# A six-block decoder kernel: order of the first transfers, waits at first use, and where the fp4 weights are turned

## The reference, cut to what matters

```python
x = _layernorm(x + _L0_attn_ref(x, Wq, Wk, Wv, Wo))            # causal self-attention with rope, 16 heads
x = _layernorm(x + _L0_xattn_ref(x, ctx, ...))                  # cross-attention, q and k normed per head
x = _layernorm(x + _L0_ffn_ref(x, w_gate, w_up, w_down))        # gated feed-forward, inputs and weights in fp4
x = _layernorm(x + _L1_attn_ref(x, ...))                        # linear attention, depthwise convolutions, MLP
x = _layernorm(x + _L1_xattn_ref(ctx, x, ...))                  # causal cross-attention
x = _layernorm(x + _L1_ffn_ref(x, ...))                         # 8 experts, top 2

def fp4_linear(x, w):                                           # inside _L0_ffn_ref
    return einsum('bsk,nk->bsn', fp4_quant_dequant(x), fp4_quant_dequant(w))   # per block of 16, along k
```

## Time and profile before

| | |
|---|---|
| median of 3 runs | 846.2 us (846.08 to 848.11) |
| the profiled execution | 849.09 us, its span 847.3 us |
| instructions | 13277 |
| PE busy | 663.4 us (78%) |
| DVE busy | 559.9 us (66%) |
| ACT busy | 350.0 us (41%) |
| POOL busy | 94.3 us (11%) |
| mean granted clock of PE | 0.894 |
| moved by DMA | 10.11 MB, 7.12 MB of it in the first 30 us |

### The profile page before, as it was taken

The page is one execution under the profiler, slowest core; times in us unless marked ns, Lnnn a source line. Parts: engine busy times, 40 slices in busy tenths (PEclk is TensorE's granted clock), DMA queues, the critical chain, the costliest instruction groups (busy, mean ns, idle before and its releaser), DMA issues.

```text
span 847.3 us, 13277 instructions
## 1 busy us (share of the span) xinstructions
PE 663.4 (78%) x5081; PEld 440.5 (52%) x5081; DVE 559.9 (66%) x1492; ACT 350.0 (41%) x568; POOL 94.3 (11%) x224
## 2 busy tenths in 40 slices
PE   1788479675889797999957965876668969889995
PEld 0557347443454374566635753564435436646663
DVE  6476667889676664554547685678967656465555
ACT  0653535221766552322227443622238546332220
POOL 0002100202102101000020020021120130100002
PEclk9999769677799898999989995796969989899998
DMA  9000100000000000000000000000000000000000
GB/s 320 17 2 14 37 1 2 0 1 0 2 1 1 1 2 1 1 1 0 1 28 2 2 1 1 2 1 1 0 2 1 1 0 2 2 0 1 1 1 25
DMA packets 8867, 10.11 MB, mean 12 GB/s; under 512 B 1240, under 2 KB 7776, under 8 KB 8288
## 3 DMA queue, kind: packets, MB, share of 16 engines
q1 hardware_dynamic: 8800, 9.22, 3.2%
HBM read 8.17 MB, written 1.05 MB: 11 GB/s over the span
## 4 chain that ended last, share of the span: by engine, by line
PE 60%; DVE 22%; ACT 11%; issue 4%; POOL 1%; another core or an unknown queue 0%; DMA 0%; SPq 0%; POOLq 0%; DVEq 0%
PE ps L780 14%; PE ps L542 8%; PE ps L771 6%; PE ps L479 6%; PE ps L498 5%; PE ps L465 2%; PE ps L725 2%; PE ps L730 2%; ACT s_k L857 2%; ACT s_probs L899 1%; DVE s_work L1060 1%; PE ps L553 1%; DVE s_r L1084 1%; PE ps L510 1%; ACT s_v L840 1%
## 5 line engine op out<-in xcount | busy, mean ns | idle before, releaser
L1011 ACT ACTIVATE s_k<-ps,eb 128x512 f32<-128x512 f32 x64 | 44.0, 687 | 136.0 <-PE ps L780 135.9
L1512 POOL TENSOR_TENSOR s_rs<-s_mv,eps 128x1 f32<-128x1 f32 x96 | 19.1, 201 | 640.1 <-DVE s_mv L1090 460.2
L1114 DVE TENSOR_REDUCE s_row_max<-ps 128x16 f32<-128x1024 f32 x48 | 58.6, 1221 | 46.8 <-PE ps L498 46.8
L1447 DVE SCALAR_TENSOR_TENSOR s_pT<-ps,eb,s_k 128x512 f32<-128x512 f32 x64 | 48.0, 749 | 57.0 <-ACT s_k L1011 53.7
L542 PE MATMUL ps<-s_v,s_pT 128*64 128x108 f32 x1536 | 82.0, 261 | 2.0 <-ACT s_headsT L890 1.7
L542 PEld LDWEIGHTS ps<-s_v,s_pT 128*64 128x64 f32 x1536 | 73.5, 138 | 11.9 <-issue 11.4
L879 ACT ACTIVATE s_pT<-ps 128x512 f32<-128x512 f32 x96 | 56.9, 595 | 51.0 <-PE ps L479 49.5
L479 PE MATMUL ps<-tabs,s_probs 128*128 128x128 f32 x384 | 64.8, 296 | 13.3 <-ACT s_probs L899 12.1
L771 PEld LDWEIGHTS ps<-wo,s_pT 128*128 128x128 f32 x512 | 61.7, 192 | 17.7 <-issue 12.4
L780 PE MATMUL ps<-s_xT,wg 128*128 128x512 f32 x128 | 69.5, 626 | 1.5 <-DVE s_pT L1447 1.1
L780 PE MATMUL ps<-s_xT,wu 128*128 128x512 f32 x128 | 68.9, 621 | 0.0
(11 more groups left out here) (220 smaller groups left out, 1130.5 us busy)
## 6 DMA issues: line engine op xcount, KB each, us to landing
mats<-in_mats SPq DMA_DIRECT2D x1, 1216.0 KB, 8.7
s_cin<-in_ctx SPq DMA_DIRECT2D x4, 256.0 KB, 4.2
s_xin<-in_x SPq DMA_DIRECT2D x4, 256.0 KB, 4.6
wg<-in_wg SPq DMA_DIRECT2D x1, 1024.0 KB
wu<-in_wu SPq DMA_DIRECT2D x1, 1024.0 KB
wo<-in_wo SPq DMA_DIRECT2D x1, 1024.0 KB
out_x<-s_x SPq DMA_DIRECT2D x4, 256.0 KB, 2.4
fc<-in_fc SPq DMA_DIRECT2D x2, 256.0 KB
```

The lines of the kernel that those rows point to most:

```text
L1011: act.activation(h.esg[:, n % 2, :], h.ps[:, 0, 0:TOK], ACT.Silu, bias=eb[:, 0, n:n + 1]).then_inc(h.e_silu, 1)
L1114: dve.tensor_reduce(h.row_max[:, t % 2, :], s3, AX, ALU.max).then_inc(h.max_here, 1)
L1447: dve.scalar_tensor_tensor(h.ehid[:, (n // 2) % 2, n % 2, :], h.ps[:, 1, 0:TOK], eb[:, 1, n:n + 1], h.esg[:, n % 2, :], ALU.add, ALU.mult) ...
```

## The change

- SP opens the pass before the transfers, and issues them in another order: `fp4_gu`, `tabs`, `cin` and `xin` of stream 0, the first 6 matrices (`MATS_FIRST`), `fp4_d`, `cin` and `xin` of stream 1, `identb`, mask, `cols`, the other 13 matrices, then the late ones. The bytes are the same.
- `late_here` and the shared counts are split into semaphores by use (`cols_here`, `more_mats_here`, `fp4_d_here`, `biases_here`, `fc_here`, `experts_here`), and each is awaited inside the loop where the data is first used. Ahead of the loop PE, ACT and DVE wait only for `tabs`, DVE also for the fp4 weights and POOL for `cols`.
- The nine transposes of the fp4 weights and ACT's three copies move into the loop, to the start of stream 0's feed-forward. They are executed in both passes.
- The fp4 weights get buffers of their own (their quantized form must last into the second pass).
- The memsets of `v2` and `hq` and the two sums for `cw1` move from DVE to POOL.

```diff
+            open_pass()
+            for h in streams:
+                sp.sem_inc(h.stored, 16)
+            sp.dma_start(fp4_gu[:, :], fp4_gu_in.rearrange("p c n -> p (c n)")).then_inc(fp4_here, 16)
+            sp.dma_start(tabs[:, :], tables_in).then_inc(tabs_here, 16)
+            load(0, 0)
+            sp.dma_start(mats[:, 0:MATS_FIRST, :], mats_in[:, 0:MATS_FIRST, :]).then_inc(mats_here, 16)
+            sp.dma_start(fp4_d[:, :], fp4_d_in).then_inc(fp4_d_here, 16)
+            load(0, 1)
+            sp.dma_start(identb[:, :], identb_in).then_inc(mask_here, 16)
+            sp.dma_start(cmask[:, :], cmask_in).then_inc(mask_here, 16)
+            sp.dma_start(cols[:, :], cols_in).then_inc(cols_here, 16)
+            sp.dma_start(mats[:, MATS_FIRST:, :], mats_in[:, MATS_FIRST:, :]).then_inc(more_mats_here, 16)
...
             def keys_ahead(h):
                 yield
+                pe.wait_ge(more_mats_here, 16)
...
+            def turn_fp4_weights(h):
+                pe.wait_ge(fp4_w_ready, 1)
+                for c in range(2 * KC):
+                    pe.transpose(h.ps[:, c // 4, tile(c % 4)], fp4_gu[:, tile(c)], ident)
+                for c in range(KC):
+                    ins = pe.transpose(h.ps[:, 2, tile(c)], fp4_d[:, tile(c)], ident)
+                ins.then_inc(fp4_w_turned, 1)
+
             def ffn(h):
+                if h is streams[0]:
+                    turn_fp4_weights(h)
                 yield
...
-            pe.wait_ge(tabs_here, 48)
-            pe.wait_ge(fp4_w_ready, 1)
-            for c in range(2 * KC):
-                pe.transpose(ps[:, c // 4, tile(c % 4)], fp4_gu[:, c, :], ident)
-            for c in range(KC):
-                ins = pe.transpose(ps[:, 2, tile(c)], fp4_d[:, tile(c)], ident)
-            ins.then_inc(fp4_w_turned, 1)
-            pe.wait_ge(fp4_w_here, 1)
-            pe.wait_ge(mask_here, 16)
-            pe.wait_ge(late_here, 16 * LATE)
+            pe.wait_ge(tabs_here, 16)
             with pe.Fori(0, PASSES):
...
+            def take_fp4_weights(h):
+                act.wait_ge(fp4_w_turned, 1)
+                act.activation(gu_w[:, 0:4 * P], h.ps[:, 0, :], ACT.Copy)
+                act.activation(gu_w[:, 4 * P:6 * P], h.ps[:, 1, 0:2 * P], ACT.Copy)
+                act.activation(d_w[:, :, :], h.ps[:, 2, 0:KC * P].rearrange("p (c n) -> p c n", n=P),
+                               ACT.Copy).then_inc(fp4_w_here, 1)
...
-            dve.wait_ge(fp4_here, 32)
+            dve.wait_ge(fp4_here, 16)
             at_once(ffn_weights(streams[0]))
-            dve.wait_ge(late_here, 16 * LATE)
+            dve.wait_ge(tabs_here, 16)
             with dve.Fori(0, PASSES):
...
             for h in streams:
+                pool.memset(h.v2_all[:, :, :], 0.0).then_inc(v_zeros_set, 1)
...
+            for h in streams:
+                pool.memset(h.hq[:, :, :], 0.0)
                 pool.memset(h.vz[:, :, :, :], 0.0).then_inc(zeros_set, 1)
+            pool.wait_ge(cols_here, 16)
...
-            pool.wait_ge(late_here, 16 * LATE)
```

More of the change, by code:

```diff
@@ L70 @@
 HEADS_NORM = 17
-LATE = 11
+MATS_FIRST = 6
 def steps(*names):
@@ L339, in decoder @@
         streams = [stream(k) for k in range(STREAMS)]
-        fp4_gu = placed(streams[1].k4, 0, 2 * KC, P)
-        fp4_d = placed(streams[1].k4, 2 * KC * P, FFN_PAD)
+        fp4_gu = sb("fp4_gu", [P, 2 * KC * P])
+        fp4_d = sb("fp4_d", [P, FFN_PAD])
         def col(name):
@@ L416, in open_pass @@
                     sp.sem_inc(t, 1)
-            sp.dma_start(tabs[:, :], tables_in).then_inc(tabs_here, 16)
-            sp.dma_start(cols[:, :], cols_in).then_inc(tabs_here, 16)
-            sp.dma_start(fp4_gu, fp4_gu_in).then_inc(fp4_here, 16)
-            sp.dma_start(fp4_d, fp4_d_in).then_inc(fp4_here, 16)
-            sp.dma_start(identb[:, :], identb_in).then_inc(tabs_here, 16)
-            for k in range(STREAMS):
-                load(0, k)
-            sp.dma_start(mats[:, :, :], mats_in).then_inc(mats_here, 16)
@@ L437, in _ @@
+            for dst, src in ((fc1[:, :], fc1_in), (fc1b[:, :], fc1b_in), (fc2[:, :, :], fc2_in)):
+                sp.dma_start(dst, src).then_inc(fc_here, 16)
+            for dst, src in ((router[:, :], router_in), (eb[:, :, :], eb_in), (wg[:, :, :], wg_in), (wu[:, :, :], wu_in),
+                             (wo[:, :, :], wo_in), (bout[:, :], bout_in)):
+                sp.dma_start(dst, src).then_inc(experts_here, 16)
             with sp.Fori(0, PASSES - 1) as c:
@@ L921, in cross_attention @@
                 yield from attention_tiles(h, 1)
+            def take_fp4_weights(h):
[4 more added lines that the diff above has]
+                               ACT.Copy).then_inc(fp4_w_here, 1)
             def ffn(h):
+                if h is streams[0]:
+                    take_fp4_weights(h)
                 yield from take_x(h, 3, 3)
@@ L1263, in ffn_weights @@
             def ffn_weights(h):
-                gu3 = fp4_gu.rearrange("p c (b k) -> p (c b) k", k=BLOCK)
+                gu3 = fp4_gu[:, :].rearrange("p (b k) -> p b k", k=BLOCK)
                 ins = yield from quantize(h, gu3, gu3, 2 * KC * P // BLOCK, once, 0)
@@ L1267, in ffn_weights @@
                 dve.wait_ge(once, 9)
-                d3 = fp4_d.rearrange("p (b k) -> p b k", k=BLOCK)
+                dve.wait_ge(fp4_d_here, 16)
+                d3 = fp4_d[:, :].rearrange("p (b k) -> p b k", k=BLOCK)
                 ins = yield from quantize(h, d3, d3, FFN_PAD // BLOCK, once, 9)
@@ L1481, in network @@
                 yield from experts(h)
-            for h in streams:
-                dve.memset(h.hq[:, :, :], 0.0)
-                dve.memset(h.v2_all[:, :, :], 0.0).then_inc(v_zeros_set, 1)
-            dve.wait_ge(v_zeros_set, 2)
-            for h in streams:
-                dve.memset(h.v2[0:S, :, 0::2, DK:DK + 1], 1.0)
-                ins = dve.memset(h.v2[S:P, :, 1::2, DK:DK + 1], 1.0)
-            ins.then_inc(v_ones_set, 1)
-            dve.wait_ge(tabs_here, 48)
-            dve.tensor_scalar(cw1[:, 0:1], col("cpe1_w1"), 1.0, None, ALU.add)
-            dve.tensor_scalar(cw1[:, 1:2], col("cpe2_w1"), 1.0, None, ALU.add).then_inc(conv_mids_set, 1)
-            dve.wait_ge(fp4_here, 32)
+            dve.wait_ge(fp4_here, 16)
             at_once(ffn_weights(streams[0]))
-            dve.wait_ge(late_here, 16 * LATE)
+            dve.wait_ge(tabs_here, 16)
             with dve.Fori(0, PASSES):
@@ L1553, in _ @@
             for h in streams:
+                pool.memset(h.v2_all[:, :, :], 0.0).then_inc(v_zeros_set, 1)
+            pool.wait_ge(v_zeros_set, 2)
+            for k, h in enumerate(streams):
+                pool.memset(h.v2[0:S, :, 0::2, DK:DK + 1], 1.0).then_inc(v_ones_set, 1)
+                pool.wait_ge(v_ones_set, 2 * k + 1)
+                pool.memset(h.v2[S:P, :, 1::2, DK:DK + 1], 1.0).then_inc(v_ones_set, 1)
+                pool.wait_ge(v_ones_set, 2 * k + 2)
+            for h in streams:
+                pool.memset(h.hq[:, :, :], 0.0)
                 pool.memset(h.vz[:, :, :, :], 0.0).then_inc(zeros_set, 1)
+            pool.wait_ge(cols_here, 16)
+            pool.tensor_scalar(cw1[:, 0:1], col("cpe1_w1"), 1.0, None, ALU.add)
+            pool.tensor_scalar(cw1[:, 1:2], col("cpe2_w1"), 1.0, None, ALU.add).then_inc(conv_mids_set, 1)
             pool.wait_ge(consts_set, 2)
-            pool.wait_ge(late_here, 16 * LATE)
             with pool.Fori(0, PASSES):
```

44 lines of the change are left out of this document (23 added, 21 removed).

## The result

The changed kernel takes **842.15 us** at the median (841.19 to 842.89, 4 runs), the kernel before on the same chip 847.15 (846.08 to 848.46, 4 runs): a ratio of 0.9936 with a 95% interval of 0.9923 to 0.9949. It is faster by 0.6%, where 833.4 was forecast, with a range of 829.5 to 839.5. The sign held and the size did not. 5 us came where 12.8 were expected.

The account below looks back on a forecast made before the run. PE was taken to carry 60% of the chain, with everything in the loop hanging on the rope product's start. From 847.3, -14.4 and +1.6 gave a span of 834.5, a median of 833.4 us; range 829.5 to 839.5.

Parts of the forecast that it names:

- Term 1: Start of the loop: without the waits ahead of it, rope product L1143 starts at 16.3 instead of 30.69, -14.4 us.
- the scale: Bytes landed against time in the kernel before, 220, 238 and 311 KB per us, used to date the new transfers.
- Rival A: Front: two DVE quantizing operations of 768 columns each wait for a POOL memset; start 1.2 later, 834.6 us; chance 0.12.
- Term 2: Nine transposes in the loop, ahead of stream 1's projection, delay it about 0.8 us a pass, twice: +1.6 us.
- Rival D: Loop: PE is granted less clock, its 508 us of chain lengthen in proportion; 859.7 us at 0.85; chance 0.03.
- B: Turn in the loop: PE is slow there, so it costs +4.0 us instead of +1.6, 835.8 us; chance 0.13.
- C: Near 23: instruction fetch held behind expert weights, 835 us; whole gain lost, 846 us; chance 0.02.

Follow-up runs that it names:

- before_turn_in: Kernel before with only the nine transposes and three copies moved into the loop, fp4 weights in own buffers, waits ahead of the loop kept: 849.15 us, ratio 1.001.
- after_third: The changed kernel unaltered, run once more: 841.15 us, ratio 0.992 to the kernel before.
- after_fill2: Changed kernel plus 80 unused PE transposes a pass, ahead of stream 1's first scores and in both cross-attentions, one wait moved earlier: 828.1 us.
- waits_in: Kernel before with the change's in-loop waits added on PE, ACT and DVE, those ahead of the loop kept: 850.0 us, ratio 1.001.

## Why the prediction was wrong

**Term 1, the front: right.** -14.4 was forecast and -14.05 came. The transfers landed 0.7 to 1.4 us later than the scale said, and DVE's ready time of 16.40 was 1.1 later than the 15.3 forecast; PE, with L591 done at 16.60, set the rope product all the same, nearly a tie. The mask, the memsets and the expert weights held nobody, as costed.

**Rival A's mechanism exists, in another place.** DVE and POOL in the kernel after:

```profile
5.13 1.33 DVE L1074 TENSOR_SCALAR s_qmax<-s_qmax 128x48 f32<-128x48 f32 x1
...
7.97 0.56 DVE L1084 TENSOR_SCALAR s_work<-s_work 128x768 int32<-128x768 int32 x1
```

```profile
4.78 0.96 POOL L1574 MEMSET s_vz<- 128x1024 f32 x1
5.67 0.74 POOL L1573 MEMSET s_hq<- 128x768 f32 x1
6.35 1.00 POOL L1574 MEMSET s_vz<- 128x1024 f32 x1
```

The kernel before has the first of these without POOL beside it:

```profile
7.54 0.19 DVE L1054 TENSOR_SCALAR s_qmax<-s_qmax 128x48 f32<-128x48 f32 x1
```

A tensor_scalar of 48 columns took 1.33 us in place of 0.19; the one of 768 columns that I feared for took its 0.56 at 7.97, when POOL was done (7.35). This is the 1.1 us that DVE was late, and it cost nothing only because PE was to come 1 us behind DVE and came 0.2 behind. The Trainium skill (SBUF — State Buffer, "SBUF: two separate sides") has a DVE operation in a two-port mode and a GpSimd operation take the shared ports in turn, the later one blocked for the whole instruction. The rows agree in part: L1074 starts at 5.13 beside the first memset above, which ends at 5.74, and itself ends at 6.46, just behind the second one's end at 6.41, so it outlasts one memset more than the one it met. The reciprocal and the product behind it, at 6.49 and 6.98 beside the third memset, take their usual 0.45 and 0.96. Whether L1074 runs in a two-port mode no row says.

**Term 2, the turn: mis-sized.** +1.6 was forecast, and the trace shows 0.25 us a pass at the place, 0.5 in all. The rows:

```profile
143.76 0.49 PE L516 MATMUL ps<-mats,s_headsT 128*128 128x128 f32 x2
...
144.09 0.82 PE L619 MATMUL ps<-tabs,fp_gu 128*128 128x128 f32 x6
...
144.75 0.49 PE L621 MATMUL ps<-tabs,fp_d 128*128 128x128 f32 x3
...
145.07 0.39 PE L516 MATMUL ps<-mats,s_headsT 128*128 128x128 f32 x2
145.27 0.60 ACT L939 ACTIVATE gu_w<-ps 128x512 f32<-128x512 f32 x1 [2.38 <-PE ps L621]
...
146.03 0.50 ACT L941 ACTIVATE d_w<-ps 128x384 f32<-128x384 f32 x1
...
146.40 0.30 ACT L904 ACTIVATE s_headsT<-ps 128x128 f32<-128x128 f32 x1
```

Stream 0's last projection starts at 143.76 here. From it to stream 1's are 145.07 - 143.76 = 1.31 us, and were 153.68 - 152.62 = 1.06 before; to the copy of stream 1's heads 146.40 - 143.76 = 2.64, and 155.01 - 152.62 = 2.39 before. So the turn makes stream 1 late by 0.25, not by 0.7 or 0.8: the nine transposes take 1.15 in place of 1.3 to 1.4, and at either end they overlap their neighbours by 0.15. At the end the profile of before_turn_in shows none of it, and the medians 0.8 to 1.4, with intervals that hold 0 as well as 1.6.

**The step that failed** is the sum itself: "inside the loop a delay on the chain moves everything behind it", and so a gain at the front was carried to the end unchanged, at an unchanged clock. Rival D had the mechanism and the right price, and got 0.03, because I asked of it only whether it could turn the sign. Its own formula, put on the medians: 508 us of chain on PE x (0.900 / 0.886 - 1) = 8.0 us. The loop grew by 819.6 - 812.7 = 6.9. With the 8.0 in it the sum gives 848.3 - 14.05 + 8.0 = 842.3 on the chip of after_third, and 841.15 was measured. For after_fill2 the formula gives 508 x (0.900 / 0.914 - 1) = -7.8, and -6.1 came, with the added transposes in it. So the formula overshoots by 1 to 2 us. And the one execution of the unaltered changed kernel at 0.901 took 834.8 us, inside the range. My argument against D, that both passes show nearly the same slices, looked at one execution; the runs of one kernel differ by 0.883 to 0.901.

**Rivals B and C** did not occur. The range missed by 2.6 us for want of one term: 1% of clock is 5 us here by that formula, and the kernel before alone scatters by 7 to 9. Two of the range's ends were also added up wrongly: of the three runs one lay 1.9 above the median (848.11), not 1.6, and 830.8 less 1 is 829.8. Put right, 839.8 is still under 842.15.

**The better version.** after_fill2, at 0.976 of the kernel before, beats both; against the changed kernel it is 828.1 to 841.2.

## What to carry to other kernels

Where PE carries most of the chain and often waits for other engines, its mean granted clock is a term of the sum: multiply the PE part of the chain by the ratio of the clocks, take the clock from several executions, and give the range what that scatter is worth, before arguing on single microseconds. A gain at the front that brings no gain at the end should send one to the clock of each stretch before looking for a new wait. And in such a kernel, dummy transposes ahead of the waits that PE sits out are a cheap trial: 80 of them in each pass, none of them useful, took 13 us off the changed kernel and 7 to 8 off the kernel before, where the reordering alone brought 5 to 7, and both together 20.

## What the runs showed that I had not expected

- **The same loop takes 807 to 822 us.** Over the 20 profiled executions the length of the loop follows the clock in the main: 822.2 at 0.882, 821.4 at 0.883 and 0.885, 818.2 at 0.888, 813.3 at 0.902, 807.3 at 0.912. Farthest off are waits_in, 813.5 at 0.890, and the kernel before, 813.5 at 0.894, where others take 815.6 to 817.7. So in kernels with the waits of before the profiled loop took 813.3 to 813.5 at anything from 0.890 to 0.902, and among the single runs of the kernel before, on the chip of after_third, those at 0.898 took 845.6 to 847.0 and those at 0.902 849.4. The mean clock is a term of the sum and not the whole of it; which part of the time at the lower clock falls on the chain no run here separates.
- **The clock fell during an idle stretch of 2.69 us**, and with transposes in that stretch it stayed at 1.00. The Trainium skill (TensorE: Matmul & The Clock Gate, "HAM oscillation — how this bites in real kernels") describes how waits between pieces of work bring the clock down, so that the next piece starts slow. The rows at L497 agree, with a wait shorter than the 3 to 5 us of the page's example.
- **Work in place of idleness lowered the time** although it stood ahead of work that was waited for: 1.91 us of L477 ahead of L510 at 92.24, itself still slow, and all the places that after_fill2 adds together 10 us over two passes.
- **Waits that are never long may move the time.** With them ahead of the loop the changed kernel took 848.6 us, with them inside 853.6, of which 1.2 is the later start (31.4 against 30.2); the rest, 3.8 us, is little above the noise of the two medians, and its way stays open.
